# Value product of a sliding-window attention split at 64 queries, with half-height products issued in pairs

## The reference, cut to what matters

```python
allowed = (j <= i) & (j > i - SLIDING_WINDOW)          # SLIDING_WINDOW = 128
scores = jnp.where(allowed[None, None, None], scores, neg)
attn = jax.nn.softmax(scores, axis=-1)
out = jnp.einsum('bhgqs,bshd->bqhgd', attn, v).reshape(B, S, N_Q_HEADS * HEAD_DIM)
return out @ wo
```

## Time and profile before

| | |
|---|---|
| Median of 3 runs | 1507.73 us (1504.65 to 1507.94) |
| Profiled execution, its own time | 1505.94 us |
| Its span, first to last instruction | 1504.1 us |
| TensorE matmul | 1476.1 us busy, 98%, 7577 instructions |
| TensorE weight load | 1227.3 us, 82% |
| VectorE | 1103.5 us, 73% |
| GpSimd | 868.4 us, 58% |
| ScalarE | 823.2 us, 55% |

### The profile page before, as it was taken

How to read it: one execution, slowest core, us unless ns; L and a number is a source line. 1 busy time by engine, 2 the same in 40 slices (tenths; PEclk the granted TensorE clock), 3 DMA queues, 4 the chain that set the end, 5 groups by cost and what they waited for, 6 DMA issues and landing times.

```text
span 1504.1 us, 27328 instructions
## 1 busy us (share of the span) xinstructions
PE 1476.1 (98%) x7577; PEld 1227.3 (82%) x7577; DVE 1103.5 (73%) x1849; ACT 823.2 (55%) x2183; POOL 868.4 (58%) x894
## 2 busy tenths in 40 slices
PE   6989999999999999999999999999999999999998
PEld 4578888888888888887888888888888888877887
DVE  6678787778787878788777878787877868773542
ACT  3555565656555656555565655565655556552331
POOL 2346565556565566669855656556664665675333
PEclk9999999999999999999999999999999999999999
DMA  9011110020201111324302020111111101153001
GB/s 315 21 36 57 36 56 28 18 73 7 72 18 56 35 56 35 104 71 134 106 16 77 7 70 21 56 35 56 35 56 35 56 28 38 60 182 127 28 29 56
DMA packets 98688, 90.20 MB, mean 60 GB/s; under 512 B 5450, under 2 KB 73042, under 8 KB 98646
## 3 DMA queue, kind: packets, MB, share of 16 engines
q1 hardware_dynamic: 97718, 87.06, 18.4%
q0 software_dynamic: 640, 2.10, 0.4%
q10 hardware_dynamic: 288, 0.53, 0.1%
HBM read 74.98 MB, written 14.69 MB: 60 GB/s over the span
## 4 chain that ended last, share of the span: by engine, by line
PE 87%; issue 4%; DVE 4%; POOL 3%; ACT 1%; DMA 1%; SPq 0%; POOLq 0%; DVEq 0%; ACTq 0%
PE pP L276 11%; PE pP L278 11%; PE pP L277 11%; PE pOp L276 8%; PE pOp L278 7%; PE pOp L277 7%; PE pS L278 4%; PE pAv L276 4%; PE pS L277 4%; PE pS L276 4%; PE pAv L277 4%; PE pAv L278 4%; PE pTr L286 3%; PE pXx L355 1%; POOL y L1310 1%
## 5 line engine op out<-in xcount | busy, mean ns | idle before, releaser
L1242 POOL TENSOR_SCALAR_AFFINE_SELECT pm<-pT 128x512 fp32r<-128x512 f32 x480 | 392.3, 850 | 477.8 <-DVE pT L865 477.7
L276 PE MATMUL pP<-hT,wp 128*128 128x512 f32 (+1 forms) x776 | 314.5, 405 | 6.9 <-DVE hT L998 4.0
L278 PE MATMUL pP<-hT,wp 128*128 128x512 f32 (+1 forms) x776 | 303.3, 391 | 0.0
L277 PE MATMUL pP<-hT,wp 128*128 128x512 f32 (+1 forms) x776 | 302.3, 390 | 0.0
L629 ACT CAST oT<-pAv 128x512 fp32r<-128x512 f32 x128 | 74.9, 585 | 283.8 <-PE pAv L278 283.8
L1255 POOL TENSOR_TENSOR rB<-rB,tab 128x512 f32<-128x512 f32 x160 | 218.3, 1376 | 16.3 <-ACT rB L652 16.2
L641 ACT ACTIVATE pr<-pS,nb 128x128 f32<-128x128 f32 x512 | 181.4, 371 | 63.3 <-DVE nb L885 63.2
L895 DVE TENSOR_TENSOR rA<-pP,tab 128x512 f32<-128x512 f32 x160 | 110.3, 689 | 131.0 <-ACT rB L652 131.0
L276 PE MATMUL pOp<-wos,oT 128*128 128x512 f32 x512 | 201.4, 393 | 3.7 <-DVE oT L860 3.4
L278 PE MATMUL pOp<-wos,oT 128*128 128x512 f32 x512 | 199.6, 390 | 0.0
L277 PE MATMUL pOp<-wos,oT 128*128 128x512 f32 x512 | 199.3, 389 | 0.0
(11 more groups left out here) (187 smaller groups left out, 3016.1 us busy)
## 6 DMA issues: line engine op xcount, KB each, us to landing
st<-in_L_attn_wq_dram SPq DMA_DIRECT2D x64, 256.0 KB, 3.5
st<-in_L_attn_wo_dram SPq DMA_DIRECT2D x64, 256.0 KB, 3.7
h_dram<-hs SPq DMA_DIRECT2D x16, 512.0 KB, 3.9
st<-in_L_attn_wk_dram SPq DMA_DIRECT2D x16, 256.0 KB, 4.2
st<-in_L_attn_wv_dram SPq DMA_DIRECT2D x16, 256.0 KB, 2.6
wm<-in_L_wmod_dram SPq DMA_DIRECT2D x4, 1024.0 KB, 10.2
xin<-in_L_attn_x_dram SPq DMA_DIRECT2D x16, 256.0 KB, 3.1
qT<-h_dram SPq DMA_DIRECT2D x2, 2048.0 KB, 10.2
```

What stands on the lines that cost most here:

```text
L276: nc.tensor.matmul(o, hi_l, hi_r, start=start, stop=False, skip_group_check=True)
L277: nc.tensor.matmul(o, hi_l, lo_r, start=False, stop=False, skip_group_check=True)
L278: return nc.tensor.matmul(o, lo_l, hi_r, start=False, stop=stop, skip_group_check=True)
L1242: last = nc.gpsimd.affine_select(out=pm[:, own, part], in_=pT[:, part], compare_op=op, fill=0.0, base=0, pattern=[[0, G], [sign, P]], chan ...
```

## The change

The probabilities' 128 queries are cut in two halves of 64 (4 heads x 64 = 256 moving columns). The first half goes to pAv[:, 0:256]. The second goes to the first half of a second bank: pOp in all units but the last, and pXx for unit 127. Each half takes a full product (128 keys, three matmuls of 256 columns) with the tile of which it needs all keys, and a product with 64 keys of the other tile: keys 0 to 63 of its own for the first half, keys 64 to 127 of the tile before for the second. These last six matmuls have 64 rows; they are issued alternately on rows 0 to 63 and on rows 64 to 127. A unit with t = 0 has only the full products. Because pOp is written now, `p_times_v` gets the wait on u_y that `out_proj` has. Taking the result out becomes two instructions of 256 columns on ScalarE and two on VectorE.

```diff
+        def av_halves(other):
+            return pAv[:, 0:256], other[:, 0:256]
...
-            def p_times_v(f, u, b):
+            def p_times_v(f, u, b, other=pOp):
                 t = u % NT
                 f.wait(u_mask, PER_U, u + 1)
                 f.wait(j_done, PER_J, JB + (6 if t >= CH else 0) + PER_J * (u // NT))
-                for own in ((1, 0) if t else (0,)):
+                f.wait(u_y, PER_U, u + 1)
+                o = av_halves(other)
+                for a in range(2):
+                    own = 1 - a if t else 0
                     tt = t - own
                     v_hi, v_lo = (kv[:, i, 1, tt * P:(tt + 1) * P] for i in range(2))
-                    last = mm3(pAv[:], v_hi, v_lo, pm[:, own, 0].rearrange("p h q -> p (h q)"),
-                               pm[:, own, 1].rearrange("p h q -> p (h q)"), own == 1 or t == 0, own == 0)
+                    p_hi, p_lo = (pm[:, own, i, :, 64 * a:64 * a + 64] for i in range(2))
+                    last = mm3(o[a], v_hi, v_lo, p_hi, p_lo, True, t == 0)
+                for v, p in ((0, 0), (0, 1), (1, 0)) if t else ():
+                    for a in range(2):
+                        rows = slice(64 * a, 64 * a + 64)
+                        own = a
+                        last = nc.tensor.matmul(o[a], kv[rows, v, 1, (t - own) * P:(t - own + 1) * P],
+                                                pm[rows, own, p, :, 64 * a:64 * a + 64],
+                                                start=False, stop=v == 1, skip_group_check=True)
                 last.then_inc(u_av, 1)
...
             out_proj(fl, -2)
-            p_times_v(fl, -1, 1)
+            pe.wait_ge(h_act, STEPS)
+            p_times_v(fl, -1, 1, pXx)
...
-            def result_hi(f, u):
+            def result_hi(f, u, other=pOp):
                 f.wait(u_av, PER_U, u + 1)
-                nc.scalar.copy(oT[:, 0].rearrange("p h q -> p (h q)"), pAv[:]).then_inc(u_ohi, 1)
+                for a, bank in enumerate(av_halves(other)):
+                    last = nc.scalar.copy(oT[:, 0, :, 64 * a:64 * a + 64], bank.rearrange("p (h q) -> p h q", h=G))
+                last.then_inc(u_ohi, 1)
...
-            def result_lo(f, u):
+            def result_lo(f, u, other=pOp):
                 f.wait(u_ohi, PER_U, u + 1)
-                nc.vector.tensor_tensor(oT[:, 1].rearrange("p h q -> p (h q)"), pAv[:],
-                                        oT[:, 0].rearrange("p h q -> p (h q)"), ALU.subtract).then_inc(u_olo, 1)
+                for a, bank in enumerate(av_halves(other)):
+                    last = nc.vector.tensor_tensor(oT[:, 1, :, 64 * a:64 * a + 64],
+                                                   bank.rearrange("p (h q) -> p h q", h=G),
+                                                   oT[:, 0, :, 64 * a:64 * a + 64], ALU.subtract)
+                last.then_inc(u_olo, 1)
```

More of the change, by code:

```diff
@@ L830, in _ @@
             p_hi(fl, -1)
-            result_hi(fl, -1)
+            result_hi(fl, -1, pXx)
             def ff_act(i):
@@ L1183, in _ @@
             add_y(fl, -2, 1)
-            result_lo(fl, -1)
+            result_lo(fl, -1, pXx)
             add_y(fl, -1, 1)
```

## The result

The changed kernel takes 1617.6 us (median of 4 runs, 1608.4 to 1618.6) against 1506.2 for the kernel before: ratio 1.073 [1.069, 1.076]. It is slower by 7%. The forecast was 1591 us and slower, with a range of 1545 to 1632. The profiled execution took 1618.6 us, 112.6 more than that of before.

The account below looks back on a forecast made before the run. PE, busy 498.4 of 500 us, was taken to bound the kernel. Matmuls -17, t = 0 units +0.3, stalls +98.3 and tail +2 gave +84 us on 1505.9: 1590, by median 1591 us; 8-in-10 range 1545 to 1632.

Parts of the forecast that it names:

- signs of being wrong: Waits for `add_y` summing to under 60 us, PE at 1.2 GHz behind them, or a unit's matmuls over 1.41 us.
- Value product: Matmuls of 112 units with t > 0: 0.15 us saved each, 17 us in all (37 to -3).
- a rival of 0.12: Pairs don't pay: changing between 128 and 64 rows empties the array, 0.32 us a unit, 36 us, 1627 us; chance 0.12.
- Tile 2: Value product at t = 2 waits 2.51 us for `add_y`, plus 0.16 us restart, in 15 heads.
- the rival of catching up: VectorE catches up after the first stall; only t = 2, t = 0 and the tail remain: +36 us, 1543 us; chance 0.08.
- Tile 3: Value product at t = 3 waits 2.16 us for `add_y` behind two weight splits, plus 0.16 us restart, in 15 heads.
- Tile 4: Value product at t = 4 waits 0.7 us for `add_y`, plus 0.16 us restart, in 15 heads.
- Tile 0: Value product at t = 0 waits 0.50 us for `add_y`, plus 0.16 us restart, in 16 heads.
- The term of 0.32 us for the four pieces: Copies at t = 0: two instructions instead of one cost 0.16 us more on VectorE and the same on ScalarE.
- a rival at 0.05: Clock falls behind thirty stalls of over 2 us, 2.5 us lost each: 75 us more, 1666 us; chance 0.05.
- the tail: Products of units 126 and 127 at the end: about 1 us each, 2 us.
- The faster one: The wait is already met when PE gets there, leaving only the saving: -17 us (to -37), 1491 us; chance 0.05.

Follow-up runs that it names:

- the early sum: Changed kernel with VectorE's `add_y` moved ahead of the weight splits and of every fourth step's last rotary product; 1511.3 us, ratio 1.003.
- the wait alone: Kernel before with only the wait on u_y put in front of the value product; products, banks and copies unchanged; 1589.7 us, ratio 1.057.
- the kernel before with the early sum: Kernel before with both moves of `add_y` (ahead of the weight splits and of the last rotary product) and nothing else; 1502.7 us, ratio 0.997.

## Why the prediction was right or wrong

Right in direction, in the main cause (the wait for `add_y`) and in its place; in size +84 us against +113 in the profiled execution, and that partly by luck, since terms that were off in both directions partly cancel. One of its own signs of being wrong came true: PE did work at 1.2 GHz behind the stalls. The other two did not (the waits sum to 63.9 us in 51, above its bound of 60 but well under the 95 foreseen, and a unit takes 1.38 us). PE's busy share is 94%, not 92%. The terms, for the 15 heads with all splits:

- *Value product, -17 us foreseen; -2 at most measured* (1.38 us against 1.40 or 1.41 from its first matmul to the transposes, but the next product is reached no earlier, 9.10 against 9.09 us at tile 1). The column counts were right: 0.12 us for a full-height matmul and for a pair. The working put the unknown of the pairs into their overlap, and took the middle; overlap turned out to be complete, as the page "TensorE: Matmul & The Clock Gate", Part 3, of the Trainium skill says. What was missing from the sum is the change of height, 0.33 us a unit, that I had as a rival of 0.12 and priced at 0.32 us. So both were true at once, and they cancel. "TensorEngine Tiling (Array Packing)", Key Properties, in the Trainium skill says that a change of mode drains the engine. The 0.33 us agree with that; the draining itself stands in no row. The error was to keep the two unknowns apart, one in the sum and one in a rival.
- *Tile 2, 2.67 us foreseen; 2.66 measured* (2.56 in front of the product, 0.10 in it). The chain from PE's turning of V through ScalarE and VectorE came back in full in each head, and the rival of catching up is refuted: the stalls of tiles 3 and 4 come in each of the 15 heads too.
- *Tile 3, 2.32 us foreseen; 1.3 measured.* The step that failed is the one that took the two weight splits at 2.32 us. In the trace of before they ran beside GpSimd's rotary products:

```profile
436.67 2.53 POOL L1255 TENSOR_TENSOR rB<-rB,tab 128x512 f32<-128x512 f32 x2
```

In the changed kernel these are over before the splits begin, and the splits take 1.29 us:

```profile
473.77 1.30 POOL L1274 TENSOR_TENSOR rB<-rB,tab 128x512 f32<-128x512 f32 x1 [1.43 <-ACT rB L668]
475.52 1.29 DVE L1052 TENSOR_TENSOR wp<-st,wp 128x512 fp32r<-128x512 f32 x2
```

That is the missing 1.0 us. A duration was carried into a place where its neighbour isn't the same. That the neighbour is the cause wasn't tried alone, but the trace of before speaks for it: the 48 splits beside which GpSimd ran nothing took 0.68 or 0.69 us each, and 14 that lay beside its product of `pr` with `rs`, 512 columns wide, took 1.52 or 1.53. Over all 96 splits the mean went from 977 ns to 823, and to 762 with the early sum.

- *Tile 4, 0.86 foreseen; 0.83 in front of the product measured.* Right in size. From one `add_y` to the next VectorE took 10.0 us, as worked out; but its wait for ScalarE's copy was 0.58 us, not 0.4, and the pieces, put at 0.3 with it, add nothing that shows: with whole copies, in the run of the wait alone, the stall is 0.85.
- *Tile 0, 0.66 foreseen; 0.34 measured* (0.24 and 0.10). The term of 0.32 us for the four pieces failed: the 0.24 is the 0.18 that the earlier trace rows show and the 0.06 of the restart, and the wait alone, with whole copies, has the same stall (0.25). For one thing, two instructions of 256 columns don't cost two durations. ScalarE's begin 0.27 us apart and VectorE's 0.34:

```profile
464.61 0.37 ACT L644 CAST oT<-pAv 128x256 fp32r<-128x256 f32 x1 [4.17 <-PE pOp L330]
464.88 0.38 ACT L644 CAST oT<-pOp 128x256 fp32r<-128x256 f32 x1
465.29 0.42 DVE L877 TENSOR_TENSOR oT<-pAv,oT 128x256 fp32r<-128x256 f32 x1 [1.49 <-ACT oT L644]
465.63 0.41 DVE L877 TENSOR_TENSOR oT<-pOp,oT 128x256 fp32r<-128x256 f32 x1
```

So ScalarE's pair lasts 0.65 us against 0.59 and VectorE's 0.75 against 0.69: 0.06 us more each, not 0.16. And these 0.12 us are made good, because ScalarE begins earlier:

```profile
430.67 0.30 PE L280 MATMUL pAv<-pm,kv 128*128 128x256 f32 x1
432.16 0.37 ACT L644 CAST oT<-pAv 128x256 fp32r<-128x256 f32 x1 [4.08 <-PE pOp L330]
...
438.83 0.67 DVE L943 TENSOR_TENSOR y<-y,pOp 128x512 f32<-128x512 f32 x1
```

The copy starts 1.49 us behind the product's first matmul, where before it was 1.60 (399.02 to 400.62), and `add_y` ends 8.83 us behind it, where before it was 8.82.

- *Clock, nothing in the sum, a rival at 0.05; about 38 us measured* (13 falls at 2.84 us, one at 1.6). This is the largest miss. The rival's price for one fall, 2.5 us, was near; its argument against, that 2.4 us is half of the 4.35 us wait of the earlier trace rows and lies in dense work, was no evidence. The wait alone shows that the same stalls can come with 6 short falls as well.

Together: the stalls, foreseen at about 100 us with the tail, were 72 us more than before by the starts in the traces, and the restarts behind them some 5; the clock added 38; the value products gave back 2. So the forecast had 23 us too much for the stalls, 38 too little for the clock and 15 too little for the value products: about 30 us too low in all, and nearer than its working. Of the rivals, "the pairs don't pay" was right about the change of height. The faster one is refuted.

## What to carry to other kernels

Before a product borrows a bank, look up where the bank's last reader ends against the new first writer, unit by unit: an engine with a quarter of its time free can still be 2.5 us late at the one place where it is needed, and here moving that one reader ahead of work that nobody awaits gave back 103 of 111 us, and made the unchanged kernel 0.3% faster too. Half-height pairs halve the matmul time but pay about 0.2 us for each change of height, so three at a time don't pay; that many of them standing together would is worked out from these figures, not tried. A stall of PE has to be priced with the clock behind it.

## What the runs showed that I had not expected

- Behind an idle time of 2.4 us the granted clock can fall from 2.4 to 1.2 GHz, at 1.6 or 2.84 us a time. Six, nine, fourteen or fifteen heads of fifteen were hit by practically the same wait, depending on work elsewhere. In the kernel before with the early sum one fall came behind a wait of 1.87 us, in the tail. Filling the wait with matmuls whose result nobody reads took all the falls at tile 2 away.
- Matmuls on rows 0 to 63 and on rows 64 to 127 overlapped even when issued three and three instead of in turns. In "TensorE: Matmul & The Clock Gate", Part 3, the Trainium skill calls the order of matmuls strictly that of the program; the run with the rows one by one shows a later one starting 0.2 us ahead of an earlier one, and here the measurement decides.
- A wait of PE of 0.14 us and its restart, 0.24 us a head together, stand in no list of PE's idle times. They show in the distance between starts, and in the weight loads' list as idle time put down to "issue".
